# A fused transformer kernel: in its two cross-attentions, the next batch's first key block moves between the last two value products, and the maxima's transposes move in front of the last key block

## The reference, cut to what matters

```python
q, k, v = query @ Wq + bq, key @ Wk + bk, value @ Wv + bv        # 16 heads of 16
attn1 = jnp.einsum('bhqd,bhkd->bhqk', qh, kh)
attn2 = jnp.einsum('bhqd,qkd->bhqk', qh, rk)                     # the first one only
attn = jax.nn.softmax((attn1 + attn2) / scale, axis=-1)          # the second one: masked scores
w1 = jnp.einsum('bhqk,bhkd->bhqd', attn, vh)
w2 = jnp.einsum('bhqk,qkd->bhqd', attn, rv)                      # the first one only
```

## Time and profile before

| | |
|---|---|
| median of 3 runs | 3038.64 us (3038.64 to 3042.05) |
| the profiled execution | 3042.65 us, its span 3040.4 us |
| TensorE busy | 2752.3 us, 91% of the span |
| VectorE, ScalarE, GpSimd busy | 1401.3, 1071.5, 478.3 us |
| granted TensorE clock, mean | 0.956 of full speed |

### The profile page before, as it was taken

How to read it: one execution, slowest core, us unless ns; L and a number is a source line. 1 busy time by engine, 2 the same in 40 slices (tenths; PEclk the granted TensorE clock), 3 DMA queues, 4 the chain that set the end, 5 groups by cost and what they waited for, 6 DMA issues and landing times. The chain is left out here.

```text
span 3040.4 us, 95394 instructions
## 1 busy us (share of the span) xinstructions
PE 2752.3 (91%) x43460; PEld 1885.8 (62%) x43460; DVE 1401.3 (46%) x2411; ACT 1071.5 (35%) x1480; POOL 478.3 (16%) x406
## 2 busy tenths in 40 slices
PE   6999999999997699988999999999868998897858
PEld 3666666666665566655666666666547777776445
DVE  3444544535445711135545454544445454444268
ACT  2333333333333321123343434434334454543123
POOL 2424233243332000001000000000001111111000
PEclk9999999999997599999999999999979999999869
DMA  2110111101100000130111111110110000000000
GB/s 84 35 35 24 39 29 29 39 25 35 35 2 12 29 28 28 42 107 26 38 29 35 34 35 34 29 40 24 43 36 3 3 4 3 4 3 5 40 31 14
DMA packets 48630, 88.96 MB, mean 29 GB/s; under 512 B 8496, under 2 KB 43120, under 8 KB 46832
## 3 DMA queue, kind: packets, MB, share of 16 engines
q1 hardware_dynamic: 48240, 82.96, 9.1%
HBM read 81.89 MB, written 1.05 MB: 27 GB/s over the span
## 5 line engine op out<-in xcount | busy, mean ns | idle before, releaser
L525 DVE TENSOR_REDUCE x_mx<-banks 128x2 f32<-128x800 f32 (+1 forms) x512 | 507.3, 993 | 305.3 <-PE banks L640 215.9
L726 PE MATMUL banks<-x_wv,x_cT 128*128 128x256 f32 (+1 forms) x1664 | 466.6, 403 | 24.2 <-DVE x_nmb L530 21.1
L584 PE MATMUL banks<-x_cT,x_wk 128*128 128x400 f32 (+1 forms) x1024 | 362.5, 510 | 18.2 <-DMA x_cT<-in_ctx 18.2
L726 PEld LDWEIGHTS banks<-x_wv,x_cT 128*128 128x128 f32 (+1 forms) x1664 | 279.0, 186 | 145.6 <-issue 76.0
L433 ACT ACTIVATE x_PT<-banks,x_kbs 128x1024 f32<-128x1024 f32 (+1 forms) x208 | 231.8, 1114 | 376.8 <-PE banks L692 376.8
L433 ACT ACTIVATE x_PT<-banks 128x1024 f32<-128x1024 f32 (+1 forms) x208 | 213.0, 1024 | 429.8 <-PE banks L692 358.7
L692 PE MATMUL banks<-x_qbd,x_kT 32*128 32x128 f32 x6656 | 294.4, 273 | 0.0
L584 PEld LDWEIGHTS banks<-x_cT,x_wk 128*128 128x128 f32 x1024 | 192.8, 192 | 163.4 <-issue 27.1
L678 PE MATMUL banks<-x_PT,x_V 128*32 128x64 f32 x13312 | 272.1, 222 | 20.7 <-ACT x_PT L433 20.7
L692 PEld LDWEIGHTS banks<-x_qbd,x_kT 32*128 32x128 f32 x6656 | 253.4, 182 | 0.0
L678 PEld LDWEIGHTS banks<-x_PT,x_V 128*32 128x32 f32 x13312 | 204.9, 109 | 73.7 <-ACT x_PT L433 25.8
(11 more groups left out here) (314 smaller groups left out, 3780.2 us busy)
## 6 DMA issues: line engine op xcount, KB each, us to landing
x_cT<-in_ctx SPq DMA_DIRECT2D x96, 400.0 KB, 3.7
x_cT<-in_ctx SPq DMA_DIRECT2D x32, 401.0 KB, 3.6
e_wu<-in_mo_up SPq DMA_DIRECT2D x9, 512.0 KB, 3.8
e_wd<-in_mo_down SPq DMA_DIRECT2D x9, 512.0 KB, 4.6
x_mrow<-in_mask_row SPq DMA_DIRECT2D x1, 3202.0 KB, 11.3
g_w<-in_db_w SPq DMA_DIRECT2D x3, 1024.0 KB, 7.4
d_wqk<-in_db_qk SPq DMA_DIRECT2D x1, 2048.0 KB, 8.1
f_wgu<-in_fp_gu SPq DMA_DIRECT2D x1, 1536.0 KB, 6.2
```

The costliest lines, as they stand in the source:

```text
L525: dve.reduce_max(mx[:, H0[k]:H0[k] + 3:2, kb], g.PS[:, first:first + 2, 0:KBS[kb]], AXX).then_inc(max_read, 1)
L584: last = pe.matmul(PJ[pb][:, 0:KBS[k]], wk[:, c, gg, :], cT[:, (p + 1) % 2, c, KB0[k]:KB0[k] + KBS[k]], start=c == 0, stop=c == KC - 1)
L726: last = pe.matmul(PJ[pb][0:CHK[c], 0:D], cT[:, p, cc, 128 * c:128 * c + CHK[c]], wv[:, cc, :], start=cc == 0, stop=cc == KC - 1)
```

## The change

TensorE: at the end of body b, between value products 11 and 12, it waits until all 16 maxima of batch b + 1 have been read, and projects key block 0 of batch b + 2. Body b + 1 then has key blocks 1 and 2, the transposes, and key block 3 behind them. ScalarE: the two copies of key block 0 come behind exponential 12 and in front of the copy of the output, with the waits that stood at the head of the body. This holds for the blocks of bodies 1 to 14 (`next_keys` gives nothing for others); the key blocks of body 0 stay in body -1.

```diff
+        def next_keys(b):
+
+            i, p = divmod(b + 1, 2)
+            if not 1 <= b + 1 <= B - 2:
+                return None
+            kinds, plans, base, stride = SECT[1 if i == 0 else 2 if i < B // 2 - 1 else 3]
+            return (Bank(base, stride, i - 1) if 0 < i < B // 2 - 1 else Bank(base)), plans[p], i, p
+
...
                 if ahead:
-                    if later(b):
-                        act.wait_ge(s_full, NCH * b)
-                        act.wait_ge(kbf_done, NKB * b)
-                    for k in range(NKB) if attend else ():
+                    for k in range(0 if b == 0 else 1, NKB) if attend else ():
                         key_block(bank, plan, p, k)
...
+                    coming = next_keys(b)
+                    if coming:
+                        act.wait_ge(s_full, NCH * (b + 1))
+                        act.wait_ge(kbf_done, NKB * (b + 1))
+                        key_block(coming[0], coming[1], coming[3], 0)
                     if rel:
                         act.wait_ge(rv_done, b + 1)
...
-                    for k in range(NKB) if attend and not (isinstance(b, int) and b == 0) else ():
+                    for k in range(1, NKB - 1) if attend and b else ():
                         key_block(bank, plan, i, p, k)
...
                     last.then_inc(full[pb], 1)
+                    if ahead and b:
+                        key_block(bank, plan, i, p, NKB - 1)
                     for c in range(NCH):
...
+                    coming = next_keys(b)
+                    if coming:
+                        pe.wait_ge(max_read, UN * (b + 2))
+                        key_block(*coming, 0)
                     attend_values(NCH - 1)
```

## The result

The changed kernel takes 3023.19 us (median of 4 runs, 3021.15 to 3024.91) against 3040.35 us (4 runs) before: a ratio of 0.994, 95% interval 0.9923 to 0.9957. That is 17.2 us less where 24.2 were forecast. 3023.19 lies inside the range of 3003 to 3025, near its upper end. Timed again on another chip the same kernel gave 0.9956 (0.9943 to 0.997), 12.9 us less.

What follows compares the result with a forecast made beforehand. TensorE was taken to bound the kernel. 14 x (0.48 + 0.68) = 16.2 us in the first cross-attention plus 14 x (0.57 + 0) = 8.0 in the second gave 24.2: 3038.6 - 24.2 = 3014.4 us, range 3003 to 3025.

Steps and rivals of the forecast that it cites:

- What bounds the kernel: TensorE, busy 2752.3 of 3040.4 us; each batch it waits for exponential 12 and for VectorE's product spreading the transposed maxima.
- Rival D: Both attentions: the two waits are no loss, later slack takes them up; nothing measurable, 3038.6 us; chance 0.05.
- Key block 0: Before value product 12: covers 0.68 and 0.77 us lost per batch, net 0.48 and 0.57 us in first and second attention.
- Rival B: At the batch boundary, key block 0 only trades one wait for another; 9.5 us gain left, 3029 us; chance 0.1.
- exposed load of 0.20 us: Head of a run of keys: cutting the run shows its weight load once more, 0.20 us per batch.
- Transposes, first attention: Transposes before key block 3 cover value projection 0's wait for the spread product: 0.68 us won per batch.
- Rival C: First attention, head of body to maximum 0: GpSimd's casts come too late; slower, 3058 us at 7 us late; chance 0.02.
- Transposes, second attention: Gain of 0.55 to 0.82 us at value projection 0 handed back at maximum 0, waiting for ScalarE's mask row; net 0.
- rival A: Second attention: the mask row does not hold maximum 0 up; 9.5 us more gain, 3004.9 us; chance 0.1.
- 0.15 for the transposes: Second attention: time by which transposes delay key block 3, 0.15 us of the mask row's 0.35 us delay.
- bound of -0.30: Second attention, low bound per batch: key block 3 later by the transposes' whole modelled 0.43 us and its weight load.
- The page on weight loads: At the cut in the keys: the skill's rule would make it free, sum 5.6 us larger; forecast kept 0.20 us exposed.

## Why the prediction was right, and where it was short

- **What bounds the kernel.** Right. Both waits were real losses: where one was covered and nothing took its place, each batch became shorter by what was lost there, less what the cover cost, to the tenth of a microsecond. Rival D (no measurable change) is out.
- **Key block 0.** Right: 0.44 and 0.53 us per batch against 0.48 and 0.57 forecast. Key block 1 does not wait for ScalarE. Rival B is out, by the kernel with key block 0 alone. The 0.04 us missing in each attention are the wait for the maxima's read. The prediction worked it out, as 0.04 us, and put it at nothing; in the traces it is there in all 28 batches. The exposed load of 0.20 us was right.
- **Transposes, first attention.** Right in kind, 0.62 against 0.68; the 0.68 stood for 0.29 us from the transposes to the keys, and it took 0.35. GpSimd's chain stays hidden: its first three casts are done by 341.42 and maximum 0 starts at 344.65 in the trace after. Rival C had no room; a longer chain was not tried.
- **Transposes, second attention.** The mechanism was named in advance, with its place and its releaser, and rival A, which denied it, is out. The size was off: "I take 0" was -0.27 us. The term that was mis-sized is "0.15 for the transposes". That pace was taken from value products, whose records stream 64 columns where a transpose streams 128; the trace after has 0.36 us from the transposes' start to the keys' (1623.44 to 1623.80), 0.35 in the first attention. With the head of the run on top, the mask row ended 0.55 us later against the other keys instead of 0.35: (1628.90 - 1623.44 - 2.69) less (1642.40 - 1640.18). That is 0.20 of the 0.27 us. The rest is 0.03 us that the working itself had and rounded away, and 0.04 us from the mask row's end to maximum 0, 0.10 instead of 0.06. The bound of -0.30, which used the record's whole 0.43 us, was the nearer one.
- **The sum.** Forecast 16.2 + 8.0 = 24.2 us; the traces give 14.9 + 3.9 = 18.9. By batch, 0.27 us are missing at that term and 0.04, 0.06 and 0.04 us at the three others: 14 x 0.41 = 5.7 us, where the spans lack 5.3; the two ways of counting differ by 0.4 us. The measured 17.2 us differ from 18.9 by less than the two stretches outside the change scatter, so that the median came this near to the sum of the traces is in part luck.
- **The page on weight loads.** The Trainium skill's rule (TensorE: Matmul & The Clock Gate, "Step-by-step: what each phase is for"), by which a weight load is pulled ahead of matmuls in flight if the row groups do not conflict or it goes to the background buffer, does not make a cut free here. In the trace after, the first load of value projection 0 does start 0.33 us ahead of its matmuls, behind keys (1626.26 and 1626.59); the first load of key block 3, behind the transposes, starts together with its matmuls (1623.80). Joining the run again won the 0.21 us of the cut. The forecast went by the row and was right to. Which of the page's two conditions fails at the cut is not shown.

## What to carry to other kernels

When work is moved to cover a wait, follow every engine's own queue to the next thing that needs it: in the second attention the transposes' move won 0.6 us at one wait and handed 0.9 back at the next, because ScalarE did an unrelated row of mask behind the delayed copies; moving that row was worth 12.6 us, and nothing before. A piece that is not cut out of a long run is the cheaper cover: each cut cost some 0.2 us. To size such a move, take the instruction that is moved and not another with smaller tiles; where its start-to-start time is hidden by a wait, as here, its record (0.43 us for 0.36) was nearer than the other's pace (0.15). And a small wait that the working gives, 0.04 us, goes into the sum.

## What the runs showed that was not expected

A wait of TensorE of 2.24 us in each of 14 batches cost about twice its growth: behind 13 of them the granted clock was 0.50 to 0.66 in the next 4 us, and the value projection took 1.63 us instead of 1.13 in the batch shown. Behind the change's 14 waits of 0.72 us the clock was 1.00. And a whole run's time scatters by stretches that the change does not touch, up to 8 us each from trace to trace, while the touched ones repeat within 0.4 us.
